# Normalised x tiles 6 to 15 transposed by transposing transfers from SyncE's queue instead of matmuls and ScalarE's copies

## The reference

```python
xn = _layernorm(x, axis=-1)                       # x: 8 x 2048 x 1024, float32
x = x + attn(xn, W_attn, b_attn, W_proj, b_proj, temperature) + ffn(xn, w_gate, w_up, w_down)

# attn: 16 heads of 64, causal softmax of q.k / (8 * temperature) + slope * (key - query)
# ffn (weights are integers, times 1/127):
h = silu(xn @ w_gate.T) * (xn @ w_up.T)           # hidden size 3072
return h @ w_down.T
```

## Time and profile before

| | |
|---|---|
| median of 3 runs | 1149.74 us (1149.16 to 1150.83) |
| the profiled execution's own time | 1151.06 us |
| its span, slowest core (core 1) | 1149.5 us |
| the other cores' spans | 1144.0 to 1146.5 us |
| PE busy | 1101.4 us (96%) |
| DVE, ACT, POOL busy | 585.8, 516.1, 266.6 us |
| transposing matmuls L739 in the prologue | 16 groups of 8 |

### The profile page before, as it was taken

How to read it: one execution, slowest core, us unless ns; L and a number is a source line. 1 busy time by engine, 2 the same in 40 slices (tenths; PEclk the granted TensorE clock), 3 DMA queues, 4 the chain that set the end, 5 groups by cost and what they waited for, 6 DMA issues and landing times.

```text
span 1149.5 us, 24412 instructions; the slowest of 8 cores (1144.0 to 1149.5 us)
## 1 busy us (share of the span) xinstructions
PE 1101.4 (96%) x7702; PEld 562.9 (49%) x7702; DVE 585.8 (51%) x1190; ACT 516.1 (45%) x933; POOL 266.6 (23%) x289
## 2 busy tenths in 40 slices
PE   3899899999999999999999999999999999999998
PEld 1344455555555555555555555555555344444443
DVE  5441766666666676676666666666773100000110
ACT  1443456655655665565565566556666200000000
POOL 6210121222221222132222112112223432222220
PEclk9999999999999999999999999999999999999999
DMA  8439033433413432153321313113521652525222
GB/s 181 134 89 178 20 61 70 75 75 66 88 35 66 80 79 65 39 89 70 65 57 29 66 43 62 34 31 69 170 61 33 220 188 74 183 74 183 74 74 74
DMA packets 57055, 98.37 MB, mean 86 GB/s; under 512 B 23284, under 2 KB 43893, under 8 KB 55846
## 3 DMA queue, kind: packets, MB, share of 16 engines
q0 software_dynamic: 7872, 35.66, 16.5%
q1 hardware_dynamic: 46178, 52.65, 15.7%
q10 hardware_dynamic: 2884, 8.50, 1.9%
HBM read 90.49 MB, written 27.26 MB: 102 GB/s over the span
## 4 chain that ended last, share of the span: by engine, by line
PE 88%; DVE 5%; issue 3%; DMA 2%; ACT 1%; POOL 1%; DVEq 0%; ACTq 0%; POOLq 0%; SPq 0%
PE ps_gu L724 25%; PE ps_dn L885 14%; PE ps_s L815 10%; PE ps_t L796 10%; PE ps_m L704 9%; PE ps_y L831 5%; PE ps_dn L880 5%; PE ps_t L764 5%; DVE cm L553 2%; DMA xstage<-xin 2%; PE ps_m L844 1%; PE ps_s L818 1%; PE ps_t L800 1%; DVE st L501 1%; DVE hst L489 1%
## 5 line engine op out<-in xcount | busy, mean ns | idle before, releaser
L553 DVE TENSOR_REDUCE cm<-ps_s 128x1 f32<-128x512 f32 (+3 forms) x640 | 379.9, 608 | 195.0 <-PE ps_s L815 112.0
L660 ACT ACTIVATE pt<-ps_t 128x512 bf16<-128x512 f32 (+1 forms) x576 | 327.2, 575 | 241.6 <-PE ps_t L796 151.3
L724 PE MATMUL ps_gu<-xnT,wubuf 128*128 128x512 bf16 x768 | 262.0, 378 | 2.3 <-DVE hst L489 2.3
L724 PE MATMUL ps_gu<-xnT,wgbuf 128*128 128x512 bf16 x768 | 261.3, 378 | 1.2 <-ACT kst L605 1.2
L815 PE MATMUL ps_s<-kx,qx 67*128 67x512 bf16 (+3 forms) x640 | 213.5, 347 | 9.7 <-DVE cm L553 8.2
L796 PE MATMUL ps_t<-qx,kx 98*128 98x512 bf16 (+3 forms) x640 | 216.4, 348 | 2.0 <-ACT pt L660 1.8
L431 POOL TENSOR_SCALAR th_s<-th_s 128x512 f32<-128x512 f32 x96 | 59.1, 616 | 621.4 <-ACT th_s L613 621.4
L885 PE MATMUL ps_dn<-wdres,hb 128*128 128x512 bf16 x768 | 168.5, 379 | 0.0
L831 PEld LDWEIGHTS ps_y<-Vt,pt 128*128 128x128 bf16 x2176 | 125.3, 97 | 81.9
L831 PE MATMUL ps_y<-Vt,pt 128*128 128x65 bf16 x2176 | 138.8, 193 | 0.0
L594 DVE SCALAR_TENSOR_TENSOR outsb<-ps_dn,xres 128x512 f32<-128x512 f32 x32 | 20.7, 686 | 205.1 <-PE ps_dn L885 205.1
(11 more groups left out here) (74 smaller groups left out, 753.8 us busy)
## 6 DMA issues: line engine op xcount, KB each, us to landing
h_sc<-hst SPq DMA_DIRECT2D x96, 128.0 KB, 1.8
hb<-h_sc SPq DMA_DIRECT2D x4, 3072.0 KB, 14.0
xstage<-xin SPq DMA_DIRECT2D x16, 512.0 KB, 6.1
xres<-xin POOLq DMA_DIRECT2D x16, 512.0 KB, 4.8
out<-outsb ACTq DMA_DIRECT2D x15, 512.0 KB, 2.7
wgbuf<-wg_r POOLq DMA_DIRECT2D x12, 512.0 KB, 6.3
wubuf<-wu_r POOLq DMA_DIRECT2D x12, 512.0 KB, 8.9
wd_sc<-wd_r POOLq DMA_DIRECT2D x12, 512.0 KB, 8.1
```

The costliest lines, as they stand in the source:

```text
L553: e.tensor_reduce(cm[:, c0:c0 + 1], ps_s[:, s % 2 * 512:s % 2 * 512 + w], AX.X, AluOpType.max, negate=True).then_inc(sem["v_mx"], 1)
L660: e.activation(pt[t % NPT][:, 0:w], ps_t[:, t % 2 * 512:t % 2 * 512 + w], AF.Exp).then_inc(sem["a_e"], 1)
L724: mm = e.matmul(ps_gu[:, r // 8 * 512:r // 8 * 512 + 512], w[:, w0:w0 + 128], xnT[:, dc * T + tb * 512:dc * T + tb * 512 + 512], start=(dc ...
```

## The change

For tiles 6 to 15 (`XT0` = 6) PE's eight transposing matmuls and ACT's copy go. In their place SP's queue issues one transposing transfer per tile, from `xn_st[k % 4]` (128 x 1024 bf16) straight into `xnT`. SP's loop now runs to i = 19: it waits for the normalising of tile i-4, issues the load of tile i (while there is one), and behind it the transpose of tile i-4. V of such a tile waits for its transfer's semaphore (`l_xt0` to `l_xt3`) instead of ACT's copy, and DVE waits for it before it overwrites the `xn_st` buffer. Tiles 0 to 5 are still transposed by PE, and DVE still waits for PE before it overwrites one of them.

```diff
+XT0 = 6
...
-            for i in range(NT):
+            for i in range(NT + 4):
                 if i >= 4:
                     e.wait_ge(sem["v_xn"], i - 3)
-                e.dma_start(out=xstage[i % 4][:, :], in_=xin[i * 128:(i + 1) * 128, :]).then_inc(
-                    sem[f"l_x{i % 4}"], 16)
+                if i < NT:
+                    e.dma_start(out=xstage[i % 4][:, :], in_=xin[i * 128:(i + 1) * 128, :]).then_inc(
+                        sem[f"l_x{i % 4}"], 16)
+                if i - 4 >= XT0:
+                    k = i - 4
+                    e.dma_start_transpose(out=xT3[:, :, k * 128:(k + 1) * 128], in_=xn_st[k % 4][:, :]
+                                          ).then_inc(sem[f"l_xt{k % 4}"], 16)
...
-                    if i > 4:
+                    if i > 4 and i - 5 < XT0:
                         e.wait_ge(sem["p_xT"], i - 4)
+                    elif i > 4:
+                        e.wait_ge(sem[f"l_xt{b}"], 16 * xt_count(i - 5))
...
-                if 2 <= i < NT + 2:
+                if 2 <= i < XT0 + 2:
                     k = i - 2
                     e.wait_ge(sem["p_xT"], k + 1)
...
-                if i < NT:
+                if i < XT0:
                     e.wait_ge(sem["v_xn"], i + 1)
...
-                    e.wait_ge(sem["a_xe"], tt + 1)
+                    if tt < XT0:
+                        e.wait_ge(sem["a_xe"], tt + 1)
+                    else:
+                        e.wait_ge(sem[f"l_xt{tt % 4}"], 16 * xt_count(tt))
```

More of the change, by code:

```diff
@@ L266, in gu_of, with xt_count @@
             return (f // 4, f % 4) if f < NF_ATT else (f // 8 * 2 + f % 2, f % 8 // 2)
+        def xt_count(k):
+            return sum(1 for i in range(XT0, k + 1) if i % 4 == k % 4)
         v_at = {i: [(i - 1, 0)] for i in range(1, 5)}
```

## The result

The changed kernel is slower: 1.0255 times the kernel before, 95% interval 1.0238 to 1.0272. Against the 1150.28 us median of the kernel before (four runs) that is 1179.6 us, 29.3 us more. The undisturbed runs are 1178.42 and 1180.08; two of its four runs had one die at a lower clock (1251.22 and 1343.14), and the ratio leaves them out. The forecast was +13.7 us (1163.5), in a range that ended at 1173. The sign was right, the size and the range were wrong.

The account below looks back on a forecast made before the run. PE's prologue chain was taken as the bound; -4.8, -0.4, -1.7, +2.1, +8.7, +6.0, +3.4 gave 13.3 us, 13.7 in the walk. Profiled 1151.06 plus 13.7, less 1.3 to the median: 1163.5 us, range 1146 to 1173.

Parts of the forecast that it names:

- What bounds it, and tiles 6 to 9: Prologue: PE, 96% busy, bounds the kernel; transposes of tiles 6 to 9 cause no wait, V of tile 9 starts at 74.4.
- One alone, 3.6 us: An eight-block transposing transfer without other traffic: 2.3 us of issue, landing 3.6 us after issue, bounds 2.4 and 4.8.
- Tile 10, a wait of 2.1 us: Prologue, after V of tile 9: PE waits 2.1 us for a transpose behind an x load, landing at 80.1; bounds 0 and 3.3.
- Tile 11, landing 14.6 us after issue: Transpose among POOL's casts: issued 77.4, 1.2 load rest + 3.6 alone + 9.8 for casts, lands 92.0; PE waits 8.7 us.
- The wait foreseen for tile 12 (6.0 us): Prologue: tile 12's transpose follows tile 11's by 11.2 us on one queue, landing at 103.2; adds 6.0 us.
- The one-for-one rival: Engines alternate one packet per queue, so tile 11's transpose outlasts casts ending at 108.8: +23.2 us, 1173 us; chance 0.15.
- The path from q of block 2 on: Prologue's end: q of block 2 from 108.7, V of tile 13 at 114.0, last q and k end at 128.2.
- Later stages: After the prologue nothing changes: weights cast by 111 are there before they are needed.
- Tile 11 early: Rival: tile 11's transpose gets through before the casts, landing at 82: +9.3 us, 1159 us; chance 0.20.
- The slow V of tile 13, -1.7: Prologue: V of tile 13, 5.30 us at the lower clock after a pause, is off the path: -1.7 us.
- The fast rival: Transposes not held up, each landing in 5.1 us among the casts: -3.0 us, 1146.8 us; chance 0.20, half without gain.
- The other price of the Trainium skill: 1309 ns per 128 x 128 through the DMA crossbar, an estimated 10.5 us for eight blocks; set aside for the trace.

## Why the prediction was right or wrong, point by point

- **What bounds it, and tiles 6 to 9.** Right. Their transposes land in 4.5 to 5.6 us, PE does not wait, and V of tile 9 starts at 75.0, forecast 74.4 plus 0.7 for the core.
- **One alone, 3.6 us.** 3.1 us: the issue takes 1.22 us for eight blocks as for four, where I had doubled it. In the forecast path this is small.
- **Tile 10, a wait of 2.1 us.** 2.74 us. Right mechanism; the landing was 5.6 us.
- **Tile 11, landing 14.6 us after issue.** This is the step that failed: the 9.8 us added for casts to 3.6 alone and 1.2 for the load. The landing took 36.7 us, so some 32 us stand where I had put 9.8, and PE waited 30.0 instead of 8.7. The wait foreseen for tile 12 (6.0 us) vanished into that one, since tile 12's transpose landed 0.9 us after tile 11's.
- **Why it failed.** I scaled 4.9 us from two YT transfers beside casts, and rejected one for one by the earlier trace rows: 48 cast packets of 2.0 us in the stretch from 306 to 316 us, against 35 packets per engine of a transpose that took 7.4 us. The stretch was too wide. The DMA views of the kernel before, from 307.6 to 311 us and from 312 to 315 us, show what it hid:

```profile
q1 hardware_dynamic: 500, 0.13, 18.5%
q0 software_dynamic: 15, 0.49, 95.7%
...
q0 software_dynamic: 32, 0.52, 88.6%
q1 hardware_dynamic: 32, 0.00, 1.0%
```

  Most of that transpose's packets (500 of about 550) were through by 311, when 15 cast packets had started. Of the few left, 32 went between 312 and 315 us against 32 of the casts, one for one. Read so, the row agrees with the rival. So does the prologue of the kernel before, in a window that I did not look at, 94 to 104 us:

```profile
q0 software_dynamic: 342, 1.67, 96.8%
q1 hardware_dynamic: 341, 0.28, 10.6%
```

  The rule of the Trainium skill that I cited and set aside (DMA: Bandwidth & Descriptors, "Queues, rings and completion order": round-robin by packet) holds in this case, 422 to 421 and 282 to 281.
- **The one-for-one rival, +23.2 us at 0.15.** It had the mechanism and was 6 us short. It let the casts end at 108.8; they end at 114.6, since it counted 27.5 us of casts from 80.2 and left out what the sum of rows already showed, 33.1 us from issue to landing of `wpj_b`. That is 5 of the 6 us. The rest is the clock: V of tiles 11 and 12 took 9.81 us where 6.9 is the full-speed time, 2.9 us more at the lower level after 30 us without work; I had taken 1.7 from the earlier trace rows.
- **The path from q of block 2 on.** Right. From the start of q of block 2 (124.85) to V of tile 13 it is 5.2 us (forecast 5.3); the transposes of tiles 14 and 15 land in 3.2 us and PE does not wait; the shift copies are hidden in the changed kernel. From there to the end it is 14.1 us, forecast 14.2.
- **Later stages.** Unchanged within 0.4 us: 28.9 us at the end of the prologue, 29.3 in the total. The sign was not luck: a transpose among casts was the forecast's own reason for the loss, and only its size was off.
- **Tile 11 early.** It did not happen. The view from 78 to 82 us has 1075 packets under 512 B, as many as one transpose has, and tile 10's landed at 81.1; so tile 11's had not begun when the casts' data did. The x load ahead of it was not through at 80.2 either: it was issued at 77.7 and took 8.7 us, to 86.4.
- **The slow V of tile 13, -1.7.** The term holds for the core shown of the kernel before. In that execution V of tile 13, or of tile 9, took 5.3 us on four of the eight cores (1, 2, 4 and 5) and 3.6 on the others, behind much the same pause, so whether the slowest core has it is partly luck.
- **The fast rival.** Wrong as priced, a landing of 5 us among the casts. With the casts out of the way its walk comes out: tile 14's transpose lands in 3.2 us, under its threshold of 5.3, and the total is 1145.67 where it had 1146.8.
- **The other price of the Trainium skill** (VectorE: DVE Perf Modes, "The three transpose paths", 1309 ns for 128 x 128): eight blocks alone land in 3.1 us, so the trace does not agree with it here either.

## What to carry to other kernels

Price a transfer that runs beside another queue by its packets per DMA engine, and not by its bytes alone: in these runs each packet waited for one of the other queue's. The 256 KB transpose here has about 1075 packets, an x load of 512 KB some 144 (46 to 50.5 us of the kernel before). So put a transpose where no long transfer is in flight, or move the long ones: the largest here, `wpj_b`, is first read at 919 us. When a row seems to speak against a mechanism, cut the window to the moment at which both queues have work before believing it.

## What the runs showed of the hardware that was not expected

- The issue of a transposing transfer is 1.22 us for eight blocks of 128 x 128, as it was for four, when the queue is empty. With the DMA engines full one issue took 31.3 us (16.7 in the run with `wpj_b` later) and blocked everything behind it on SP.
- Two transposes in flight together from one queue, issued 1.3 us apart with nothing else running, land in 3.1 and 3.2 us. Of three issued 2.2 and 2.6 us apart, the first behind an x load, each landed in 5.8, 4.6 and 3.1 us.
- The 64 KB shift copies from `kst` to `kx` took 21.5 us at the median when issued together with the casts and behind them, 15.5 in the kernel before, and 2.0 once the casts were spread out.
- After 30 us without matmuls the granted clock was 0.50 (the 1.2 GHz level) until about 120 us, with matmuls running again from 115; pauses of 1.7 to 2.7 us at 75 and 81 us in the same kernel cost nothing. In the kernel before, pauses of about 2 us were followed by the lower level on four of the eight cores (V of a tile in 5.3 us) and by none on the other four (3.6).
